# Seven computed chunks per image instead of five, with one bank for transposed taps and two for the turns

## The chip, the cores and the metric

The kernel runs on one core of a Trainium2 chip, in float32. The metric is the device time of one execution in microseconds (us), lower is better. The engines are PE (TensorE, matrix products into PSUM banks), DVE (VectorE), ACT (ScalarE), POOL (GpSimd, which here only issues gathers) and SP (SyncE, which issues the other DMAs). Each runs its own list of instructions in a fixed order, and they wait for one another by semaphores.

## The reference

Sixteen images of 64 channels and 64 x 64 pixels pass through two residual blocks. The first has a depthwise 3 x 3 convolution whose kernels are computed per image; the second has a deformable 3 x 3 convolution:

```python
x = x + _L0_conv_ref(_gn(x), ...)   # 1x1, per-image depthwise 3x3, y * tanh(softplus(y)), 1x1
x = x + _L1_conv_ref(_gn(x), ...)

# _L1_conv_ref:
offset = _conv2d(x, w_off, b_off)                     # 18 values per pixel
mask = jax.nn.sigmoid(_conv2d(x, w_mask, b_mask))     # 9 values per pixel
xd = _deform_conv(x, offset, mask, w_def)             # 9 taps, each bilinear from 4 gathered pixels
cat = jnp.concatenate([xd, offset, mask], axis=1)
z = jnp.einsum('bihw,oi->bohw', cat, w_1x1[:, :, 0, 0]) + b_1x1[None, :, None, None]
return jax.nn.silu(z * inv[None, :, None, None] + (bn_beta - bn_mean * inv)[None, :, None, None])
```

## The kernel before

**Chunks.** An image is 8 chunks (`NCH`) of 512 pixels. Chunk g of image b has number q = 8 b + g. While the deformable convolution of image b is sampled chunk by chunk, the work that prepares images b + 1 and b + 2 is done in between.

**Sampling by gathers.** For each of the nine taps of a chunk POOL issues four indirect DMAs (L505), each of which fetches, for 128 pixels, the 2 x 2 patch of the table into `gat`. DVE multiplies a tap by its bilinear weights (L1367) and sums the corners (L1346, into `pairs`, the ninth tap into `single`). Two taps make a pair. PE transposes it (`transposes`, L690) into `tap_ps`, ACT copies that to `val` (L1035), and PE multiplies it by the weights into `z_ps` (`product`, L696). At the chunk's end ACT applies the Silu (L1045) and DVE adds the result to x (`finish`, L1408). `gat` holds one chunk: POOL may fetch tap k of chunk q only when PE has transposed the corresponding pair of chunk q - 1; the waits stand at k = 0, 2, 4, 6 and 7 (`THROTTLE`).

**The computed tap.** In some chunks (`HATS`: 0 to 4, in image 0 `HATS0`: 3 and 4; internally "hat") the ninth tap isn't gathered but computed from a coarse part of the table that SP loads once for each image. Such a chunk has 32 gathers instead of 36. In the chunk ahead of it, PE spreads a coordinate or the mask over all partitions three times (`hat_y` L740, `hat_x` L747, `hat_mask` L754, here called the three spreads, all in `xh_ps`), DVE subtracts (`hat_part`, L1378) and weighs (`hat_weigh`, L1385), and at that chunk's end it writes five selections (`hat_select`, L1394). In the chunk itself ACT makes four maps of line weights (`hat_rows`), and PE does four **turns** (`hat_up`, L771): five matmuls of 128 x 512 each, into one bank. Float32 matmuls stand as two in the trace, so a turn is x10. DVE multiplies each turn by its line weights (`hat_post`, L1401), and PE adds that to `z_ps` (`hat_out`). Turn t + 1 waits for `hat_post` of turn t, since all turns share the bank `yo_ps`.

**Order.** Tables written out by hand set the order of the work. An entry is (units, step): the step is done when that many taps of the chunk have passed. `PLAN_BLOCK0` serves chunks 1 to 3 (first block of the next image: `convolve`, `project`, `residual`), `PLAN_NORM` chunk 4 (group norm), `PLAN_PREPARE` chunks 5 to 7. Chunks 5 and 6 make offsets (`offsets`, L645), pixel coordinates (`to_pixels`, L660, into `yo_ps`) and the table (`to_table`, L612) of the next image; chunk 7 its points and, for the image after it, the depthwise kernels (`kernel_taps` L548, `kernels` L1193) and hidden layer (`hidden`, L569). `PLAN_HAT` places the steps of a computed tap and `PLAN_NEXT_HAT` those ahead of it; each engine takes from them the steps that it has. PE takes a pair's transposes at even taps, as soon as DVE has summed both.

**Banks.** `tap_ps` has two banks, used in turn by the pairs; `yo_ps` serves turns and pixels, `xh_ps` the spreads.

## Time and profile before

| | us |
|---|---|
| median of 3 runs | 5573.58 |
| lowest, highest | 5561.91, 5580.89 |
| profiled execution, its own time | 5569.03 |
| its span | 5567.2 |

| engine | busy in the span |
|---|---|
| DVE | 80% |
| PE | 76% |
| POOL | 74%, without the time between its issues |
| ACT | 45% |

The profile shows one execution. Its page gives sums over the whole run; the stretches (windows) give the same for a part of it; the timeline shows each instruction with the idle time of the engine before it and what ended that. PEclk is the granted share of PE's full clock of 2.4 GHz; it is 1.0 or 0.5 at any moment. Image 9 stands for the others below: it begins at 3203.84 us and ends at 3542.68 us, by DVE's copies of the chunks' weights (L1355).

### The profile page before, as it was taken

How to read it: one execution, taken by the hardware profiler on the slowest of the kernel's cores; microseconds unless marked ns; L12 is line 12 of the kernel's file. 1: busy time of each engine (PE TensorE's matmuls, PEld its weight loads, DVE VectorE, ACT ScalarE, POOL GpSimd, SP SyncE). 2: the span in 40 equal slices, each digit the busy share in tenths (PEclk: the TensorE clock that was granted, in tenths of full speed). 3: DMA queues.
4: the chain of work that ended last, by engine and by line, in shares of the span. 5: the costliest groups of instructions: out<-in, count | busy, mean ns of one | idle time of the engine just before them, and what ended most of it. 6: DMA issues, size and time to landing. Idle time of an engine off the chain costs nothing.

```text
span 5567.2 us, 43350 instructions
## 1 busy us (share of the span) xinstructions
PE 4232.8 (76%) x13878; PEld 1852.8 (33%) x13878; DVE 4433.4 (80%) x5166; ACT 2478.1 (45%) x3420; POOL 4109.3 (74%) x4307
## 2 busy tenths in 40 slices
PE   8586777777777787777877778787787777778682
PEld 3233333333333333333333333333333333333231
DVE  5887869779697887978879797786978878788664
ACT  3354445445444444445544454454444444445221
POOL 1777777777777777777777777777777777777776
PEclk8686868879687786878868688696877868778685
...
GB/s 106 103 118 135 106 132 122 126 130 112 143 106 133 122 111 140 107 132 123 120 135 106 132 123 123 132 107 148 107 130 123 111 144 107 132 115 119 122 108 100
DMA packets 284052, 675.58 MB, mean 121 GB/s; under 512 B 77215, under 2 KB 119082, under 8 KB 281578
## 3 DMA queue, kind: packets, MB, share of 16 engines
...
## 4 chain that ended last, share of the span: by engine, by line
DVE 29%; POOL 28%; PE 26%; issue 13%; DMA 3%; ACT 1%; DVEq 0%; POOLq 0%; ACTq 0%; SPq 0%
POOL gat L505 28%; PE yo_ps L771 14%; DVE conv_ps L1237 7%; DVE gat L1367 5%; DVE pairs L1346 5%; DVE hat_s L1394 3%; DMA gat<-patch_table,ixu 3%; PE z_ps L696 3%; PE tap_ps L690 2%; DVE hat_wy L1401 1%; DVE xb L1258 1%; PE conv_ps L569 1%; DVE stat L1260 1%; PE xh_ps L754 1%; DVE conv_ps L1234 1%
## 5 line engine op out<-in xcount | busy, mean ns | idle before, releaser
L505 POOL DMA_INDIRECT gat<-patch_table,ixu x4300 | 4101.3, 954 | 1445.6 <-issue 1292.9
L771 PE MATMUL yo_ps<-hat_s,hat_image 128*128 128x512 f32 x3080 | 1660.9, 694 | 472.4 <-DVE hat_wy L1401 453.4
L1367 DVE TENSOR_TENSOR gat<-gat,wgt_ps 128x1024 f32<-128x1024 f32 x1075 | 1303.2, 1215 | 635.3 <-DMA gat<-patch_table,ixu 629.0
L1346 DVE TENSOR_REDUCE pairs<-gat 128x256 f32<-128x1024 f32 x1024 | 1239.7, 1211 | 0.0
L771 PEld LDWEIGHTS yo_ps<-hat_s,hat_image 128*128 128x128 f32 x3080 | 659.4, 223 | 1372.8 <-issue 871.5
L1035 ACT ACTIVATE val<-tap_ps 128x512 f32<-128x512 f32 x512 | 303.5, 593 | 1100.1 <-PE tap_ps L690 1099.7
L690 PE MATMUL tap_ps<-ident,pairs 128*128 128x128 f32 x2048 | 395.6, 325 | 470.4 <-DVE pairs L1346 470.3
L1237 DVE SCALAR_TENSOR_TENSOR conv_ps<-xh,kb,conv_ps 128x1024 f32<-128x1024 f32 x480 | 617.6, 1287 | 12.7
L690 PEld LDWEIGHTS tap_ps<-ident,pairs 128*128 128x128 f32 x2048 | 266.9, 163 | 759.5 <-DVE pairs L1346 618.3
L696 PE MATMUL z_ps<-val,w_pair 128*64 128x256 f32 x2048 | 425.2, 502 | 10.2 <-ACT val L1035 2.1
L645 PE MATMUL conv_ps<-np,w_om 128*41 128x512 f32 x1440 | 394.3, 706 | 39.4 <-ACT cat L994 39.4
L1075 ACT ACTIVATE hat_h<-xh_ps,hat_c 128x512 f32<-128x512 f32 x77 | 52.9, 688 | 800.3 <-PE xh_ps L747 800.3
L1401 DVE TENSOR_TENSOR hat_wy<-yo_ps,hat_wy 128x512 f32<-128x512 f32 x308 | 211.4, 686 | 215.0 <-PE yo_ps L771 210.8
L569 PE MATMUL conv_ps<-n_z,w_in 64*128 64x512 f32 x224 | 211.1, 1095 | 66.8 <-ACT n_z L899 60.3
L1394 DVE SCALAR_TENSOR_TENSOR hat_s<-hat_g,hat_c,xh_ps 128x512 f32<-128x512 f32 x385 | 259.6, 740 | 0.0
L991 ACT ACTIVATE cat<-conv_ps,vec 32x512 f32<-32x512 f32 x121 | 82.1, 679 | 326.4 <-PE conv_ps L645 322.4
L1059 ACT ACTIVATE hat_wy<-hat_wy,one_c 128x512 f32<-128x512 f32 x308 | 222.3, 722 | 10.0
L1057 ACT ACTIVATE hat_wy<-hat_d,hat_c 128x512 f32<-128x512 f32 x308 | 217.5, 706 | 0.0
L696 PE MATMUL z_ps<-hat_wy,w_hat 128*64 128x256 f32 x1232 | 202.1, 408 | 0.0
L645 PEld LDWEIGHTS conv_ps<-np,w_om 128*41 128x41 f32 x1440 | 97.4, 137 | 300.4 <-issue 254.6
L696 PEld LDWEIGHTS z_ps<-val,w_pair 128*64 128x64 f32 x2048 | 120.0, 161 | 182.6 <-issue 137.1
L612 PE MATMUL conv_ps<-ident,np 128*128 128x128 f32 x480 | 112.0, 371 | 85.6 <-ACT rec L970 85.6
...
## 6 DMA issues: line engine op xcount, KB each, us to landing
gat<-patch_table,ixu POOLq DMA_INDIRECT x4300
...
patch_table<-rec SPq DMA_DIRECT2D x120, 256.0 KB, 2.4
...
out<-n_z SPq DMA_DIRECT2D x128, 128.0 KB
...
```

The source lines that it names most:

```text
L505: pool.indirect_dma_start(gat[:, k, t * 2 * REC:(t + 1) * 2 * REC], None, table_rows, bass.IndirectOffsetOnAxis(ixu[:, i, k, t:t + 1], 0)) ...
L569: pe.matmul(hidden_ps(n, j)[:, :], w_in[C:, :], n0[C:, j, :], start=True, stop=True).then_inc(xh_mm, 1)
L645: m = pe.matmul(om_ps[C * j:C * j + OM, :], w_om[:, i, :], inner(np1, 0, 128, (s * 2 + j) * ROWS + 2 * (i // 3), i % 3), start=(i == 0), s ...
L690: m = pe.transpose(tap_ps[p % 2][:, t * 128:(t + 1) * 128], pairs[:, p, t, :] if p < PAIRS else single[:, t, :], ident[:, :])
L696: m = pe.matmul(z_ps[C * j:C * j + C, 0:CH // 2], weights, columns[:, j * CH // 2:(j + 1) * CH // 2], start=start, stop=stop)
L771: m = pe.matmul(hat_sum[:, :], hat_image[:, i, t, :], hat_s[:, i, :], start=(i == 0), stop=(i == HI - 1))
L1035: act.activation(val[:, p % 2, :], tap_ps[p % 2][:, :], ACT.Copy).then_inc(tap_done, 1)
L1237: dve.scalar_tensor_tensor(acc, src, kb[:, k:k + 1], acc, ALU.mult, ALU.add).then_inc(conv_sum, 1)
L1346: dve.tensor_reduce(total, gat[:, k, :].rearrange("p (t x c h) -> p t c x h", t=TILES, x=2, h=2), mybir.AxisListType.XY, ALU.add).then_inc ...
L1367: dve.tensor_tensor(patch, patch, wk.rearrange("p (n h) -> p n h", h=2).unsqueeze(2).to_broadcast([128, TILES * 2, C, 2]), ALU.mult).then_ ...
L1394: dve.scalar_tensor_tensor(hat_s[:, i, :], hat_g[:, :], hat_c[:, i:i + 1], hat_rows_ps[:, :], ALU.is_equal, ALU.mult).then_inc(hat_chosen, 1)
L1401: dve.tensor_tensor(hat_wy[:, t, :], hat_sum[:, :], hat_wy[:, t, :], ALU.mult).then_inc(hat_scaled, 1)
```

## The change

More chunks are computed: 0 to 6 of each image, and 3 to 6 of image 0. All transposed pairs go to one bank, `tap_ps[0]`, so a pair's transposes now wait for ACT's copy of the pair before. The other bank, `tap_ps[1]`, joins `yo_ps` for the turns: even turns use `yo_ps`, odd ones `tap_ps[1]`, and turn t waits for `hat_post` of turn t - 2. Pixels stay in `yo_ps`, and only even turns mind them. In a chunk without a computed tap the product of the last pair now comes ahead of the transposes of `single`. The tables are written anew: turns 0 and 1 at units 1 and 2, turns 2 and 3 at 5 and 6, and in chunks 5 to 7 offsets, table, pixels and points at other units.

```diff
@@ -44,8 +44,8 @@
 PXC = 2 * KK + KK
 GRID_X, GRID_Y = OM, OM + 1
 CROW = OM + 2
-HATS0 = (3, 4)
-HATS = (0, 1, 2, 3, 4)
+HATS0 = (3, 4, 5, 6)
+HATS = (0, 1, 2, 3, 4, 5, 6)
 HG = 7
 HT = 4
 HI = 5
@@ -65,15 +65,15 @@
 )
 PLAN_NORM = ((1, "project"), (3, "residual"), (4, "group_mean"), (5, "group_var"), (6, "normalise"), (8, "finish"))
 PLAN_PREPARE = (
-    ((1, "last_row"), (1, "offsets 0"), (2, "to_table 0"), (2, "x_stats 0"), (3, "to_table 1"), (4, "offsets 1"), (4, "to_pixels 0"),
-     (5, "to_table 2"), (5, "x_stats 1"), (6, "to_table 3"), (7, "to_pixels 1"), (8, "to_table 4"), (8, "finish")),
-    ((1, "offsets 2"), (2, "to_table 5"), (2, "points 0"), (3, "offsets 3"), (3, "to_pixels 2"), (4, "points 1"), (4, "to_table 6"),
-     (5, "x_stats 2"), (5, "to_table 7"), (6, "points 2"), (6, "to_pixels 3"), (7, "x_stats 3"), (8, "finish")),
-    ((1, "x_mean"), (1, "points 3"), (2, "x_var"), (2, "points 4"), (2, "next_indices"), (3, "x_norm"), (3, "points 5"),
+    ((1, "last_row"), (2, "offsets 0"), (2, "to_table 0"), (2, "x_stats 0"), (3, "to_table 1"), (4, "to_pixels 0"), (4, "to_table 2"),
+     (5, "offsets 1"), (5, "x_stats 1"), (6, "to_table 3"), (7, "to_table 4"), (8, "to_pixels 1"), (8, "finish")),
+    ((2, "offsets 2"), (2, "to_table 5"), (2, "points 0"), (4, "to_pixels 2"), (4, "points 1"), (4, "to_table 6"),
+     (5, "offsets 3"), (5, "x_stats 2"), (6, "points 2"), (6, "to_table 7"), (7, "x_stats 3"), (8, "to_pixels 3"), (8, "finish")),
+    ((1, "x_mean"), (2, "points 3"), (2, "x_var"), (3, "points 4"), (3, "next_indices"), (3, "x_norm"), (4, "points 5"),
      (4, "hidden_units"), (5, "kernel_taps"), (6, "kernels"), (6, "hidden 0"), (7, "hidden 1"), (8, "hidden 2"), (8, "finish"), (KK, "hidden 3")),
 )
-PLAN_HAT = ((1, "hat_rows"), (1, "hat_up 0"), (3, "hat_post 0"), (3, "hat_up 1"), (5, "hat_post 1"), (5, "hat_out 0"), (5, "hat_up 2"),
-            (6, "hat_out 1"), (7, "hat_post 2"), (7, "hat_up 3"), (8, "hat_out 2"), (KK, "hat_post 3"))
+PLAN_HAT = ((1, "hat_rows"), (1, "hat_up 0"), (2, "hat_up 1"), (3, "hat_post 0"), (4, "hat_post 1"), (5, "hat_out 0"), (5, "hat_up 2"),
+            (6, "hat_out 1"), (6, "hat_up 3"), (7, "hat_post 2"), (8, "hat_post 3"), (8, "hat_out 2"))
 PLAN_NEXT_HAT = ((1, "hat_y"), (3, "hat_part"), (4, "hat_x"), (6, "hat_mask"), (8, "hat_weigh"), (KK, "hat_select"))
 
 
@@ -361,7 +361,7 @@
 
             return C if n % 2 == 0 else 0
 
-        hat_sum, hat_rows_ps = yo_ps, xh_ps
+        hat_sums, hat_rows_ps = (yo_ps, tap_ps[1]), xh_ps
 
         def inner(buf, lo, hi, r0, c0):
 
@@ -686,8 +686,9 @@
             def transposes(q, p):
 
                 pe.wait_ge(summed, KK + taps_before(q) + min(2 * p + 2, KK))
+                pe.wait_ge(tap_done, copies_before(q) + p + 2)
                 for t in range(TILES if p < PAIRS else TILES // 2):
-                    m = pe.transpose(tap_ps[p % 2][:, t * 128:(t + 1) * 128], pairs[:, p, t, :] if p < PAIRS else single[:, t, :], ident[:, :])
+                    m = pe.transpose(tap_ps[0][:, t * 128:(t + 1) * 128], pairs[:, p, t, :] if p < PAIRS else single[:, t, :], ident[:, :])
                 m.then_inc(tap_mm, 1)
 
             def to_z(weights, columns, start=False, stop=False):
@@ -723,9 +724,9 @@
                         if k > 2:
                             product(q, k // 2 - 2)
                     if k == KK - 1:
+                        product(q, PAIRS - 1)
                         if not has_hat(q):
                             transposes(q, PAIRS)
-                        product(q, PAIRS - 1)
                         last_products(b, g)
 
             def hat_y(q):
@@ -762,13 +763,14 @@
                         pe.wait_ge(cleared, 3)
                         pe.wait_ge(om_done, NCH)
                     pe.wait_ge(hat_chosen, HI * h + HI)
-                if h + t > 0:
-                    pe.wait_ge(hat_scaled, HT * h + t)
-                if after_px:
-                    pe.wait_ge(px_done, after_px.pop())
-                ups[0] = HT * h + t + 1
+                if h > 0 or t > 1:
+                    pe.wait_ge(hat_scaled, HT * h + t - 1)
+                if t % 2 == 0:
+                    if after_px:
+                        pe.wait_ge(px_done, after_px.pop())
+                    ups[0] = HT * h + t + 1
                 for i in range(HI):
-                    m = pe.matmul(hat_sum[:, :], hat_image[:, i, t, :], hat_s[:, i, :], start=(i == 0), stop=(i == HI - 1))
+                    m = pe.matmul(hat_sums[t % 2][:, :], hat_image[:, i, t, :], hat_s[:, i, :], start=(i == 0), stop=(i == HI - 1))
                 m.then_inc(hat_mm, 1)
 
             def hat_out(q, t):
@@ -1032,12 +1034,12 @@
                     if k % 2 == 0 and k > 0:
                         p = k // 2 - 1
                         act.wait_ge(tap_mm, GROUPS + groups_before(q) + p + 1)
-                        act.activation(val[:, p % 2, :], tap_ps[p % 2][:, :], ACT.Copy).then_inc(tap_done, 1)
+                        act.activation(val[:, p % 2, :], tap_ps[0][:, :], ACT.Copy).then_inc(tap_done, 1)
                     if k == KK - 1 and not has_hat(q):
                         act.wait_ge(tap_mm, GROUPS + groups_before(q) + GROUPS)
                         for h in range(2):
                             act.activation(val[0:C, PAIRS % 2, :].rearrange("p (t h x) -> p t h x", h=2, x=128)[:, :, h, :],
-                                           tap_ps[PAIRS % 2][C * h:C * h + C, 0:CH // 2].rearrange("p (t x) -> p t x", x=128), ACT.Copy).then_inc(tap_done, 1)
+                                           tap_ps[0][C * h:C * h + C, 0:CH // 2].rearrange("p (t x) -> p t x", x=128), ACT.Copy).then_inc(tap_done, 1)
                 if hi < KK:
                     return
                 act.wait_ge(z_mm, q + 1)
@@ -1398,7 +1400,7 @@
                 h = hats_before(q)
                 dve.wait_ge(hat_mm, HT * h + t + 1)
                 dve.wait_ge(hat_lines, 2 * (HT * h + t) + 2)
-                dve.tensor_tensor(hat_wy[:, t, :], hat_sum[:, :], hat_wy[:, t, :], ALU.mult).then_inc(hat_scaled, 1)
+                dve.tensor_tensor(hat_wy[:, t, :], hat_sums[t % 2][:, :], hat_wy[:, t, :], ALU.mult).then_inc(hat_scaled, 1)
 
             def finish(b, g):
 
```

In chunk 2 of an image, PE's list was, from the first spread for the next chunk to turn 2:

```order
L740 MATMUL xh_ps<-cat,hat_sel 128x512
L771 MATMUL yo_ps<-hat_s,hat_image 128x512 x5
L589 MATMUL conv2_ps<-uc,w_out 128x512 x2
L690 MATMUL tap_ps0<-ident,pairs 128x128 x4
L771 MATMUL yo_ps<-hat_s,hat_image 128x512 x5
L747 MATMUL xh_ps<-cat,hat_sel 128x512
L690 MATMUL tap_ps1<-ident,pairs 128x128 x4
L696 MATMUL z_ps<-cat,w_cat 64x256 x2
L696 MATMUL z_ps<-val,w_pair 64x256 x2
L696 MATMUL z_ps<-hat_wy,w_hat 64x256 x2
L771 MATMUL yo_ps<-hat_s,hat_image 128x512 x5
```

and is now:

```order
L741 MATMUL xh_ps<-cat,hat_sel 128x512
L773 MATMUL yo_ps<-hat_s,hat_image 128x512 x5
L589 MATMUL conv2_ps<-uc,w_out 128x512 x2
L773 MATMUL tap_ps1<-hat_s,hat_image 128x512 x5
L691 MATMUL tap_ps0<-ident,pairs 128x128 x4
L748 MATMUL xh_ps<-cat,hat_sel 128x512
L691 MATMUL tap_ps0<-ident,pairs 128x128 x4
L697 MATMUL z_ps<-cat,w_cat 64x256 x2
L697 MATMUL z_ps<-val,w_pair 64x256 x2
L697 MATMUL z_ps<-hat_wy,w_hat 64x256 x2
L773 MATMUL yo_ps<-hat_s,hat_image 128x512 x5
```

Turn 1 has moved ahead of the first pair's transposes; the second pair's transposes now stand between it and turn 2, with the second spread.

In chunk 5, from chunk 4's last product to the pixels and the first product of its own, PE's list was (L602 is the table's last row, L645 offsets, L612 table, L690 or L691 transposes, L660 pixels):

```order
L696 MATMUL z_ps<-hat_wy,w_hat 64x256 x2
L602 MATMUL conv2_ps<-ident,np1 97x128 x2
L645 MATMUL conv2_ps<-np1,w_om 41x512 x12
L612 MATMUL conv2_ps<-ident,np1 128x128 x4
L690 MATMUL tap_ps0<-ident,pairs 128x128 x4
L612 MATMUL conv2_ps<-ident,np1 128x128 x4
L645 MATMUL conv2_ps<-np1,w_om 41x512 x12
L660 MATMUL yo_ps<-to_px,cat 128x27 x8
L690 MATMUL tap_ps1<-ident,pairs 128x128 x4
L696 MATMUL z_ps<-cat,w_cat 64x256 x2
```

and is now:

```order
L697 MATMUL z_ps<-hat_wy,w_hat 64x256 x2
L741 MATMUL xh_ps<-cat,hat_sel 128x512
L773 MATMUL yo_ps<-hat_s,hat_image 128x512 x5
L602 MATMUL conv2_ps<-ident,np1 97x128 x2
L645 MATMUL conv2_ps<-np1,w_om 41x512 x12
L612 MATMUL conv2_ps<-ident,np1 128x128 x4
L773 MATMUL tap_ps1<-hat_s,hat_image 128x512 x5
L691 MATMUL tap_ps0<-ident,pairs 128x128 x4
L612 MATMUL conv2_ps<-ident,np1 128x128 x4
L660 MATMUL yo_ps<-to_px,cat 128x27 x8
L612 MATMUL conv2_ps<-ident,np1 128x128 x4
L748 MATMUL xh_ps<-cat,hat_sel 128x512
```

A spread for chunk 6 and two turns have come in ahead of the first pair's transposes, and the second offsets (L645) have moved behind the first products. Turns 2 and 3 follow later in the chunk.

## Rows read from the trace of the kernel before

**Rows 1.** The page: busy time by engine, and the gathers among the costliest groups.

```profile
PE 4232.8 (76%) x13878; PEld 1852.8 (33%) x13878; DVE 4433.4 (80%) x5166; ACT 2478.1 (45%) x3420; POOL 4109.3 (74%) x4307
...
L505 POOL DMA_INDIRECT gat<-patch_table,ixu x4300 | 4101.3, 954 | 1445.6 <-issue 1292.9
```

**Rows 2.** Waits of POOL, whole run: us in total, times, longest.

```profile
POOL gat L505 <- PE tap_ps L690: 42.0, 59, 4.4
```

**Rows 3.** Windows, chunks and image 9: us; PE, PEld, DVE, ACT, POOL busy (x); PEclk.

```profile
3203.84:3245.88 42.04, 36.40 (x102) 14.81 (x102) 36.82 (x39) 23.00 (x31) 31.68 (x35) 0.82 0.60 157
3245.88:3290.97 45.09, 34.83 (x102) 14.27 (x102) 41.15 (x44) 21.26 (x28) 34.11 (x37) 0.85 0.37 108
3290.97:3334.61 43.64, 33.00 (x102) 13.54 (x102) 41.16 (x44) 21.28 (x28) 32.98 (x36) 0.92 0.37 109
3334.61:3379.72 45.11, 34.83 (x102) 14.27 (x102) 41.17 (x45) 21.27 (x28) 34.09 (x36) 0.85 0.35 108
3379.72:3411.82 32.10, 28.39 (x85) 12.29 (x86) 26.32 (x35) 16.72 (x17) 24.44 (x26) 0.89 0.37 109
3411.82:3441.44 29.62, 24.56 (x120) 11.38 (x122) 24.25 (x26) 15.95 (x26) 22.48 (x24) 0.81 0.42 133
3441.44:3487.01 45.57, 35.81 (x162) 18.18 (x158) 30.88 (x43) 16.33 (x29) 34.51 (x36) 0.69 0.49 146
3487.01:3542.68 55.67, 37.87 (x101) 17.05 (x100) 35.08 (x54) 22.23 (x36) 42.15 (x45) 0.53 0.46 123
3203.84:3542.68 338.84, 265.68 (x872) 115.79 (x872) 276.83 (x319) 158.04 (x218) 256.44 (x271) 0.78 0.43 124
```

**Rows 4.** Waits in chunk 7 of image 9.

```profile
DVE gat L1367 <- DMA gat<-patch_table,ixu: 12.0, 5, 4.0
```

**Rows 5.** Timeline of DVE, chunk 2 of image 9: start, us, instruction, idle before.

```profile
3313.12 1.21 DVE L1346 TENSOR_REDUCE pairs<-gat 128x256 f32<-128x1024 f32 x1
...
3330.72 0.69 DVE L1401 TENSOR_TENSOR hat_wy<-yo_ps,hat_wy 128x512 f32<-128x512 f32 x1 [2.03 <-PE yo_ps L771]
3331.32 3.37 DVE L1394 SCALAR_TENSOR_TENSOR hat_s<-hat_g,hat_c,xh_ps 128x512 f32<-128x512 f32 x5
```

**Rows 6.** Timeline of PE, chunk 2 of image 9: turns 0 and 1.

```profile
3292.17 4.56 PE L771 MATMUL yo_ps<-hat_s,hat_image 128*128 128x512 f32 x10
...
3305.43 7.23 PE L771 MATMUL yo_ps<-hat_s,hat_image 128*128 128x512 f32 x10 [6.54 <-DVE hat_wy L1401]
3312.59 1.12 PE L747 MATMUL xh_ps<-cat,hat_sel 43*128 43x512 f32 x2
```

**Rows 7.** Timeline of PE, chunk 5 of image 9: offsets, table, transposes, pixels.

```profile
3414.43 5.35 PE L645 MATMUL conv_ps<-np,w_om 128*41 128x512 f32 x24
3419.72 0.75 PE L612 MATMUL conv_ps<-ident,np 128*128 128x128 f32 x4
3420.30 0.60 PE L690 MATMUL tap_ps<-ident,pairs 128*128 128x128 f32 x4
...
3433.33 1.96 PE L660 MATMUL yo_ps<-to_px,cat 41*128 41x27 f32 x16
```

**Rows 8.** Window of PE's small matmuls in chunks 5 and 6; clock after the engines.

```profile
3437.20:3451.30 14.10, 13.04 (x54) 8.60 (x53) 8.00 (x9) 5.44 (x11) 10.75 (x12) 0.50 0.54 172
```

**Rows 9.** Timeline of PE, chunk 7 of image 9: transposes, kernel taps, hidden.

```profile
3511.26 1.11 PE L690 MATMUL tap_ps<-ident,pairs 128*128 128x128 f32 x4 [2.56 <-DVE pairs L1346]
...
3514.41 4.00 PE L548 MATMUL conv_ps<-hcx,kg_w 128*128 128x1 f32 x18
3518.86 3.75 PE L569 MATMUL conv_ps<-n_z,w_in 64*128 64x512 f32 x4 [0.46 <-DVE kb L1193]
```

**Rows 10.** Timeline of DVE, chunk 7 of image 9.

```profile
3491.32 1.22 DVE L1367 TENSOR_TENSOR gat<-gat,wgt_ps 128x1024 f32<-128x1024 f32 x1 [4.01 <-DMA gat<-patch_table,ixu]
...
3518.45 0.17 DVE L1193 TENSOR_TENSOR kb<-conv_ps,kg_b 128x9 f32<-128x9 f32 x1 [1.43 <-PE conv_ps L548]
...
3542.07 0.68 DVE L1408 TENSOR_TENSOR n_z<-n_z,xb 64x512 f32<-64x512 f32 x1 [6.21 <-ACT n_z L1045]
```

## Prediction

> **What bounds the kernel now.** I read the page's busy line first: DVE 80%, PE 76%, POOL 74% [rows 1]. That hides the bound. POOL's gathers are busy 4101.3 us and stand 1292.9 us in "issue" [rows 1], together 5394.2 of 5567.2 us; over the whole run POOL waits only 42.0 us for PE's transposes [rows 2]. One gather thus costs 5394.2 / 4300 = 1.254 us. An image with five computed chunks has 268 gathers, 336.1 us; image 9 took 338.84 [rows 3]. POOL paces the kernel.
>
> The stretches of image 9 show the second resource [rows 3]. They begin where DVE copies a chunk's weights. POOL needs 40.1 us for a computed chunk (32 gathers) and 45.1 for another (36). Chunks 0 to 3 take DVE 42.0 to 45.1, chunks 4 and 5 only 32.1 and 29.6: DVE and PE fall behind POOL by some 16 us over four chunks and win it back in two light ones. In chunks 6 and 7 DVE has caught up and waits for gathers, 12.0 us of chunk 7 [rows 4]. The patch buffer holds about one chunk, which is how far POOL can lead. So the kernel is fast as long as DVE and PE together need less than POOL over an image, and the change touches both sides.
>
> **What the change takes from POOL.** 2 more chunks in 15 images and 2 more in image 0 are computed: 32 chunks x 4 gathers x 1.254 us = 160.5 us, 10.0 us an image. That is all there is to gain while POOL bounds; then an image takes 260 x 1.254 = 326.1 us.
>
> **What it puts on DVE and PE.** A computed chunk loses two DVE passes of 1.21 us (multiply and sum of the last tap). It gains four turn products of 0.69, and the chunk before it one pass each for part and weight (0.6) and five selections, 3.37 [rows 5]. That is about +5.1 us of DVE for each, 10.2 an image on 276.8 [rows 3]: not yet over the line. On PE it gains four turns of 4.56 us at the full clock [rows 6], 3 spreads of 1.1, and 4 products of some 0.6 for the 2 that it loses, about 22 us; at the half clock nearly twice that. PE was busy 265.7 of 338.8 us [rows 3], so with two more such chunks it is busy some 310.
>
> Since both engines work in a fixed order, I walk the chunks in the new order.
>
> *Chunk 5.* This is the term that decides. It was the lightest chunk; PE spent 24.6 of 29.6 us on two conversions of offsets, five table chunks and two of pixels [rows 3]. At the full clock PE's list now is: 4 turns at 4.4 from start to start = 17.6; three spreads 3.2; two offsets at 5.3 = 10.6; two pixel groups at 1.9 = 3.8; five table chunks and the last row at about 0.6 = 3.4; four transposes and nine products at 0.58 = 7.5 [rows 7]. Sum 46.1 us. All its inputs are ready early, so PE runs through. DVE ends when turn 3 and then the mask spread are done (39.5), and then weighs 0.6, sums tap 7 1.1 and selects 3.3: 44.6 us. That is 15.0 more than before, and more than POOL's 40.1.
>
> The clock comes on top. PE was busy 13.04 of 14.10 us in a stretch of transposes, products and pixels in chunks 5 and 6, and was granted 0.50 throughout, 1.2 of 2.4 GHz [rows 8]. Chunk 5 now has two such stretches between turns and offsets: to_table 1 to product 0, and from the mask spread to the chunk's end. A turn after such a stretch is slower: 7.23 against 4.56 us after 6.54 us of idling [rows 6]. Bounds: 44.6 us if none is lost, 49 if both stretches and the turns behind them lose 2 us each. I take 46.5, **+16.9**.
>
> By the Trainium skill, "TensorE: Matmul & The Clock Gate", Part 4: PE-mode transpose, transposes do not bring up the full clock as other matmuls do. The row on the 14.10 us agrees, though other small matmuls stand in it too. By that rule chunk 5 would take the upper bound, 49 us, and without it 44.6.
>
> *Chunk 6* gets four turns, and no next selection behind it. PE starts 1.4 us late; turns 0, offsets, table and turn 1 end at 16, turn 3 at 36.6; DVE's last product and sum follow: 38.5 at the full clock, 43.6 with the same losses. Before it was held by gathers to 45.6. I take 40.5, **-5.1**.
>
> *Chunk 4* now prepares chunk 5: +4.6 us of DVE; but turn 1 no longer stands ahead of the group mean. Walked: turn 3 ends at 28.6, then the mask, and 5.0 us of weighing, summing and selecting: 34.8; with slow turns 38.4. I take 36.0, **+3.9**.
>
> *Chunks 1 to 3.* DVE's own work is 41.2 us, the chunks took 45.1, 43.6 and 45.1 [rows 3]; the rest is DVE's wait for turns, as 2.03 us for turn 3 [rows 5]. This is what the pairs are to remove. Turns 0 and 1 now run back to back and end at 11.7 us, before DVE needs them. But PE then idles, but for one spread, until DVE has summed tap 3: the sum starts at 22.15 us [rows 5], 22.75 with the earlier product, and ends at 23.9. Then come transposes, products, turn 2 (26.2 to 30.6), turn 3 (to 35.6) and the mask (36.7), and DVE ends at 41.9. After an idle of 7.9 us I expect the half clock, as turn 1 had before [rows 6]: 1.7 us more for the small matmuls and 1.5 to 2.7 for turn 2. Then it ends at 45.6. The slow turn has only moved from turn 1, where DVE had time, to turn 2, where it has none. Bounds 41.9 and 45.6; I take 44.6, **0**. Chunk 0, without residual, 41.0, **-1.0**.
>
> *Chunk 7* is held by gathers no longer. Before, the transposes of taps 2 and 3 began at 3511.26, 24.2 us into it, of which DVE had waited 4.01 for gathers: without that, 20.2. From there to DVE's addition of the kernel bias went 3518.45 - 3511.26 = 7.2 us at the half clock, and on to the end of the image 24.2 (three hidden pairs at 3.75 us, then the last sum, ScalarE and a 6.21 us wait of DVE) [rows 9, 10]. The new order puts the last transpose behind the product before it, 1.2 more: a transpose and its copies in a row. 20.2 + 7.2 + 24.2 + 1.2 = 52.8, **-2.9**. Only a warm PE would shorten it.
>
> **Sum.** 41.0 + 3 x 44.6 + 36.0 + 46.5 + 40.5 + 52.8 = 350.6 us an image, against 338.8: +11.8. It is over POOL's 326.1, so POOL now waits for PE. For images 0 to 14 that is +177. The last image has no work for a next one: it runs at POOL's pace, saves its 10 us, and lets POOL's larger lead, by estimate 13 us (between 0 and 25), run off: -23. So 5569.0 + 177 - 23 = 5723 us. The median of the runs is 4.6 us above the profiled one: 5728.
>
> The single bank for transposes costs nothing: ScalarE's copy of a pair (0.6 us) is done long before the next pair's sums, two taps of 2.26 us later. It would show only where PE is late and pairs follow one another.
>
> **Rivals.**
> *All at the full clock.* If PE, denser now, keeps it through chunks 0 to 6: 39.5 + 3 x 41.9 + 34.8 + 44.6 + 38.5 + 52.8 = 335.9, or -2.9 an image: 5569 - 44 - 23 + 5 = 5507, faster. For it: in chunks 2 and 4 the granted share was already 0.92 and 0.89. Against: every idle of over 6 us and the small matmuls cost it [rows 6, 8]. It decides at an average of 338 us an image. If chunk 7 also came to the full clock (hidden pairs at half of 3.75) POOL would bound again at 326.1 and the time would be near 5400.
>
> *All losses at once.* Chunks 42, 3 x 45.6, 38.4, 49, 43.6, 52.8 = 362.6: +357 - 23 + 5, or about 5908.
>
> *The two cancel.* 338 to 340 us an image. It needs chunks 1 to 3 at 43 and chunk 5 at 44.6: 5545 to 5590, no difference.
>
> *The second bank does not help.* If DVE's waits for turns stay as before everywhere, chunks 0 to 3 keep their 42 to 45 us: that is my forecast within 1 us, so it is not told apart by time, only by whose turn DVE waits for.
>
> **How the numbers follow.** My forecast, slower by 1% or more, has 0.60; all losses 0.08; cancelled 0.11; full clock 0.21, with POOL-bound in it at 0.03. Range: from 5510, near the full clock, to 5830, where the average image is 358 us; outside I leave some 0.10 each. About 0.3% (17 us) is what a measurement can tell. Faster 0.21, within 0.3% 0.09, slower 0.70.
>
> **What would show it.** Right: POOL's wait for PE's transposes rises from 42 us to over 250; DVE's waits for gathers in chunks 5 to 7 vanish; chunk 5 takes 45 to 49 us and is PE's; in chunks 1 to 3 PE's idle before turn 1 is gone and one before the second pair's transposes stands there; DVE ends an image with over 10 us of waiting for ScalarE. Wrong: a clock over 0.85 with chunk 5 under 44 us, POOL still without waits, or chunk 7 under 48 us.

## The result, and the profile after

The changed kernel takes 6133.54 us (median of 4 runs, 6132.76 to 6134.91) against 5569.53 us of the kernel before in the same runs: ratio 1.1011, 95% interval 1.099 to 1.1032. It is slower, as forecast, but by 564 us where the forecast said some 160. The time lies above the range.

The page after, busy time by engine and the gathers' group, answers to [rows 1]:

```profile
PE 4941.4 (81%) x15670; PEld 2149.9 (35%) x15670; DVE 4582.3 (75%) x5454; ACT 2725.8 (44%) x3740; POOL 3968.1 (65%) x4179
...
L505 POOL DMA_INDIRECT gat<-patch_table,ixu x4172 | 3960.1, 949 | 2150.6 <-issue 1193.2
```

POOL's wait for PE, whole run (us in total, times, longest), answers to [rows 2]:

```profile
POOL gat L505 <- PE tap_ps L691: 843.3, 254, 6.2
```

POOL's own work as listed fell from 5394.2 to 3960.1 + 1193.2 = 5153.3 us, but it now waits 843.3 us for PE's transposes, where it waited 42.0. (Part of the fall is only in the listing: a gather that waits for PE has no "issue" entry of 0.3 us. 270 gathers have none now, 60 had none before.) The bound has moved from POOL to PE and DVE. The windows of image 9, columns as in [rows 3], show where:

```profile
3546.62:3589.40 42.78, 35.70 (x94) 14.91 (x94) 36.92 (x38) 19.50 (x27) 29.19 (x32) 0.78 0.57 147
3589.40:3640.88 51.48, 37.38 (x102) 15.47 (x102) 41.34 (x45) 21.38 (x28) 30.23 (x33) 0.77 0.28 84
3640.88:3692.12 51.24, 37.20 (x102) 15.40 (x102) 41.34 (x45) 21.38 (x28) 30.20 (x33) 0.77 0.28 85
3692.12:3743.32 51.20, 37.18 (x102) 15.40 (x102) 41.33 (x44) 21.37 (x28) 30.28 (x33) 0.77 0.28 85
3743.32:3787.37 44.05, 38.87 (x114) 16.21 (x114) 31.00 (x43) 25.64 (x28) 30.24 (x33) 0.81 0.33 99
3787.37:3834.91 47.54, 47.41 (x192) 21.91 (x192) 29.06 (x35) 23.15 (x39) 30.22 (x33) 0.93 0.40 121
3834.91:3874.89 39.98, 39.89 (x168) 18.00 (x164) 30.64 (x45) 19.43 (x31) 28.18 (x30) 0.96 0.39 122
3874.89:3927.14 52.25, 36.74 (x117) 17.86 (x116) 34.68 (x54) 21.89 (x35) 39.67 (x41) 0.57 0.46 129
```

The image takes 380.5 us, 41.7 more than before. Chunks 5, 6 and 7 came out as forecast (47.5, 40.0, 52.3 for 46.5, 40.5, 52.8), and chunk 0 within 2 us. Chunks 1 to 3 take 51.3 us each where I had 44.6 and an upper bound of 45.6, and chunk 4 takes 44.1 for 36.0. In chunks 1 to 3 neither engine is full: DVE works 41.3 of 51.2 us, PE 37.2. So the two wait for each other by turns. Two of DVE's three largest waits, whole run, columns as for POOL's:

```profile
DVE hat_wy L1403 <- PE yo_ps L773: 368.8, 104, 12.1
DVE xb L1260 <- PE conv_ps L589: 336.1, 60, 6.4
```

The second is new: 60 times 5.6 us, four in each image, for the projection (L589) that the residual (L1260) needs. In the kernel before it was 17.4 us in all, 13 times. From the end of chunk 2 of image 9 into chunk 3 (DVE starts chunk 3 at 3692.12) the timelines read, PE first:

```profile
3686.92 0.66 PE L691 MATMUL tap_ps<-ident,pairs 128*128 128x128 f32 x4
...
3688.97 0.66 PE L691 MATMUL tap_ps<-ident,pairs 128*128 128x128 f32 x4 [0.38 <-DVE pairs L1348]
3689.55 0.65 PE L697 MATMUL z_ps<-val,w_pair 128*64 128x256 f32 x4
3693.64 1.12 PE L697 MATMUL z_ps<-val,w_pair 128*64 128x256 f32 x4 [3.43 <-ACT val L1037]
...
3695.54 2.07 PE L741 MATMUL xh_ps<-cat,hat_sel 43*128 43x512 f32 x2
3697.55 6.65 PE L773 MATMUL yo_ps<-hat_s,hat_image 128*128 128x512 f32 x10
3704.03 1.88 PE L589 MATMUL conv_ps<-uc,w_out 128*128 128x512 f32 x4
```

ACT, same stretch:

```profile
3687.61 0.60 ACT L1037 ACTIVATE val<-tap_ps 128x512 f32<-128x512 f32 x1 [9.32 <-PE tap_ps L691]
3688.23 1.28 ACT L930 ACT_TABLE_LOAD   x1
3689.52 1.15 ACT L930 ACTIVATE uc<-uc,one_c 128x1024 f32<-128x1024 f32 x1
3690.75 1.28 ACT L940 ACT_TABLE_LOAD   x1
3692.04 1.06 ACT L940 ACTIVATE uc<-uc 128x1024 f32<-128x1024 f32 x1
3693.00 0.58 ACT L1037 ACTIVATE val<-tap_ps 128x512 f32<-128x512 f32 x1
```

DVE, at the start of chunk 3:

```profile
3698.11 1.21 DVE L1348 TENSOR_REDUCE pairs<-gat 128x256 f32<-128x1024 f32 x1
3705.09 0.75 DVE L1260 SCALAR_TENSOR_TENSOR xb<-conv_ps,vec,xb 128x512 f32<-128x512 f32 x1 [5.77 <-PE conv_ps L589]
```

The fourth pair's transposes are done at 3689.6, but ACT can't copy them: it does the activation's ln (L930) and tanh (L940) first, with a table load of 1.28 us for each, 4.8 us together. PE stands 3.43 us for the copy. After that the granted clock is 0.50 (window 3693.60 to 3700.00), and back at 1.00 from 3705: the spread takes 2.07 us for 1.12, turn 0 6.65 for 4.56. Behind them stands the projection, and behind that DVE. In the kernel before ACT had the same queue:

```profile
3325.64 0.60 ACT L1035 ACTIVATE val<-tap_ps 128x512 f32<-128x512 f32 x1 [3.74 <-PE tap_ps L690]
3326.26 1.28 ACT L928 ACT_TABLE_LOAD   x1
...
3330.07 1.06 ACT L938 ACTIVATE uc<-uc 128x1024 f32<-128x1024 f32 x1
3331.88 0.60 ACT L1035 ACTIVATE val<-tap_ps 128x512 f32<-128x512 f32 x1 [0.76 <-PE tap_ps L690]
```

There turn 3 stood between the two transposes. It gave ACT 6.2 us from copy to copy, enough for 4.8 of activation and 0.6 of copy, and ACT even waited 0.76. The new table puts turn 3 ahead of the third pair's transposes, so the two pairs follow within 2.05 us, and the cover is gone.

My theory after the result: **ACT's queue** (ln and tanh between the two copies) costs some 6 us in each of chunks 1 to 4. Rivals: **too much work** (the two more computed chunks wear down POOL's lead and the rest follows), **the banks** (one bank for transposes makes pairs wait for ACT's copies), and **turn 0 ahead of the projection**, by its place alone.

### The profile page after: what moved, and what is told of

Read it like the earlier page. It is cut to its first block, busy times and chain, and to the rows that moved or that the text cites. A ratio compares the mean times of both kernels' runs of the same rounds, so it can differ in the third digit from the quotient of the medians.

```text
span 6131.3 us, 48264 instructions
## 1 busy us (share of the span) xinstructions
PE 4941.4 (81%) x15670; PEld 2149.9 (35%) x15670; DVE 4582.3 (75%) x5454; ACT 2725.8 (44%) x3740; POOL 3968.1 (65%) x4179
## 4 chain that ended last, share of the span: by engine, by line
PE 59%; DVE 24%; ACT 7%; issue 5%; POOL 4%; DMA 0%; DVEq 0%; ACTq 0%; POOLq 0%; SPq 0%
PE yo_ps L773 18%; PE tap_ps L773 10%; PE z_ps L697 9%; PE conv_ps L645 5%; DVE gat L1369 5%; DVE pairs L1348 5%; DVE conv_ps L1239 4%; PE tap_ps L691 4%; POOL gat L505 4%; PE conv_ps L569 3%; PE xh_ps L741 2%; PE xh_ps L755 2%; DVE hat_wy L1403 2%; DVE xb L1260 1%; DVE stat L1262 1%
## 5 line engine op out<-in xcount | busy, mean ns | idle before, releaser
L505 POOL DMA_INDIRECT gat<-patch_table,ixu x4172 | 3960.1, 949 | 2150.6 <-issue 1193.2
L773 PE MATMUL yo_ps<-hat_s,hat_image 128*128 128x512 f32 x2180 | 1280.1, 746 | 0.9 <-issue 0.9
L773 PE MATMUL tap_ps<-hat_s,hat_image 128*128 128x512 f32 x2180 | 982.5, 597 | 0.0
L691 PE MATMUL tap_ps<-ident,pairs 128*128 128x128 f32 x2048 | 397.9, 327 | 667.4 <-DVE pairs L1348 665.9
L773 PEld LDWEIGHTS yo_ps<-hat_s,hat_image 128*128 128x128 f32 x2180 | 509.3, 245 | 798.6 <-issue 798.6
L691 PEld LDWEIGHTS tap_ps<-ident,pairs 128*128 128x128 f32 x2048 | 269.3, 163 | 1019.3 <-DVE pairs L1348 821.9
L773 PEld LDWEIGHTS tap_ps<-hat_s,hat_image 128*128 128x128 f32 x2180 | 403.2, 190 | 496.9 <-issue 485.3
L1403 DVE TENSOR_TENSOR hat_wy<-tap_ps,hat_wy 128x512 f32<-128x512 f32 x218 | 149.2, 684 | 319.4 <-PE tap_ps L773 319.4
L1396 DVE SCALAR_TENSOR_TENSOR hat_s<-hat_g,hat_c,xh_ps 128x512 f32<-128x512 f32 x545 | 367.4, 740 | 0.0
L645 PE MATMUL conv_ps<-np,w_om 128*41 128x512 f32 x1440 | 342.2, 627 | 0.0
L1260 DVE SCALAR_TENSOR_TENSOR xb<-conv_ps,vec,xb 128x512 f32<-128x512 f32 x120 | 89.1, 743 | 336.1 <-PE conv_ps L589 336.1
L697 PE MATMUL z_ps<-hat_wy,w_hat 128*64 128x256 f32 x1744 | 338.6, 474 | 0.0
L1061 ACT ACTIVATE hat_wy<-hat_wy,one_c 128x512 f32<-128x512 f32 x436 | 314.6, 722 | 14.1
L1059 ACT ACTIVATE hat_wy<-hat_d,hat_c 128x512 f32<-128x512 f32 x436 | 307.8, 706 | 0.0
```

The lines of the kernel that those rows point to most:

```text
L505: pool.indirect_dma_start(gat[:, k, t * 2 * REC:(t + 1) * 2 * REC], None, table_rows, bass.IndirectOffsetOnAxis(ixu[:, i, k, t:t + 1], 0)) ...
L645: m = pe.matmul(om_ps[C * j:C * j + OM, :], w_om[:, i, :], inner(np1, 0, 128, (s * 2 + j) * ROWS + 2 * (i // 3), i % 3), start=(i == 0), s ...
L691: m = pe.transpose(tap_ps[0][:, t * 128:(t + 1) * 128], pairs[:, p, t, :] if p < PAIRS else single[:, t, :], ident[:, :])
L697: m = pe.matmul(z_ps[C * j:C * j + C, 0:CH // 2], weights, columns[:, j * CH // 2:(j + 1) * CH // 2], start=start, stop=stop)
L773: m = pe.matmul(hat_sums[t % 2][:, :], hat_image[:, i, t, :], hat_s[:, i, :], start=(i == 0), stop=(i == HI - 1))
L1061: act.activation(hat_wy[:, t, :], hat_wy[:, t, :], ACT.Relu, bias=one_c[:, :], scale=-1.0).then_inc(hat_lines, 1)
```

## The experiments

Medians over images 1 to 13 of the time of each chunk, in us. Each ratio is to runs of the kernel before taken beside that kernel; their medians lie between 5557 and 5570 us, so times of different rows are compared to some 12 us.

| kernel | 0 | 1 | 2 | 3 | 4 | 5 | 6 | 7 | us | ratio to before, 95% | POOL waits for tap_ps |
|---|---|---|---|---|---|---|---|---|---|---|---|
| before | 41.2 | 45.1 | 43.6 | 45.1 | 32.1 | 29.7 | 45.4 | 55.6 | 5569.53 | | 42.0 |
| after | 42.8 | 51.5 | 51.2 | 51.2 | 44.0 | 47.5 | 40.0 | 52.2 | 6133.54 | 1.099 to 1.1032 | 843.3 |
| e1_early_ln | 42.0 | 44.6 | 44.5 | 44.4 | 39.3 | 47.5 | 38.6 | 51.7 | 5759.04 | 1.0311 to 1.0372 | 434.5 |
| e2_five_hats | 41.9 | 50.6 | 51.2 | 51.2 | 36.3 | 30.3 | 45.4 | 59.1 | 5955.43 | 1.0663 to 1.0725 | 480.5 |
| e3_old_tables | 41.4 | 44.9 | 46.3 | 44.7 | 37.5 | 51.8 | 47.9 | 52.4 | 5963.52 | 1.0678 to 1.074 | 658.9 |
| e6_project_first | 42.6 | 45.3 | 44.6 | 46.2 | 40.6 | 47.5 | 39.9 | 52.1 | 5836.59 | 1.045 to 1.0512 | 510.4 |
| f4_turn3_late | 42.1 | 44.7 | 46.8 | 45.0 | 39.6 | 48.0 | 38.0 | 51.9 | 5791.04 | 1.0372 to 1.0433 | 472.3 |
| f1_five_early | 41.8 | 44.5 | 44.4 | 44.4 | 34.6 | 31.5 | 45.2 | 59.1 | 5674.67 | 1.0164 to 1.0223 | 162.6 |
| f3_one_bank_early | 45.5 | 44.6 | 44.5 | 44.6 | 40.2 | 47.5 | 40.5 | 52.1 | 5843.50 | 1.0466 to 1.0527 | 519.2 |
| f5_fill | 39.6 | 43.2 | 42.0 | 43.2 | 39.4 | 47.6 | 38.6 | 51.8 | 5660.70 | 1.0139 to 1.0198 | 339.2 |
| f2_six_early | 42.3 | 44.9 | 44.5 | 44.4 | 34.6 | 41.1 | 45.0 | 52.2 | 5695.67 | 1.0212 to 1.0273 | 273.1 |
| b1_hat6 | 41.6 | 43.6 | 45.2 | 43.6 | 30.8 | 39.2 | 54.8 | 51.7 | 5733.93 | 1.0274 to 1.0359 | 332.7 |
| b3_hat6_fill | 41.2 | 43.6 | 45.2 | 43.6 | 30.8 | 39.2 | 54.8 | 51.7 | 5723.99 | 1.0265 to 1.0329 | 330.7 |
| b2_fill | 41.7 | 43.6 | 45.1 | 43.6 | 30.8 | 30.4 | 45.4 | 55.4 | 5551.52 | 0.9965 to 0.9996 | 45.0 |

### ln and tanh ahead of the copies (e1_early_ln)

```diff
 PLAN_BLOCK0 = (..., (6, "exp"),
-               (7, "ln"), (8, "tanh"), (8, "finish"))
+               (6, "ln"), (6, "tanh"), (8, "finish"))
```

(The same in `PLAN_FIRST`.)

> The changed kernel with one thing moved: ScalarE's ln and tanh of the next image's first block come at unit 6, right behind exp, instead of at 7 and 8, so ahead of its copy of the third transposed pair. Theory Q (queue): in chunks 0 to 3 the third pair's transposes stand behind turns 2 and 3, ln and tanh with their table loads (4.8 us) then stand between ScalarE's copies of the third and the fourth pair, PE's last product waits 3.43 us for the fourth copy, and the next chunk's projection comes late for the residual, for which DVE waits 5.8 us in each of chunks 1 to 4. Then the 3.4 us wait goes, DVE's wait shrinks to 2 to 3 us, an image falls from 379 to about 365 us and the time to some 5930 us. Theory L (load): PE simply has too much work with seven computed chunks; then the time stays within 1% of 6134 us.

Measured 5759.04 us: one edit of two numbers takes back 374 of the 564 us, nearly twice the 200 that I had expected. Chunks 1 to 3 fall to 44.5, chunk 4 to 39.3. ACT and PE at the same place, end of chunk 2 of image 9, ACT first:

```profile
3446.57 1.28 ACT L940 ACT_TABLE_LOAD   x1
3447.86 1.06 ACT L940 ACTIVATE uc<-uc 128x1024 f32<-128x1024 f32 x1
3452.29 0.60 ACT L1037 ACTIVATE val<-tap_ps 128x512 f32<-128x512 f32 x1 [3.37 <-PE tap_ps L691]
3454.33 0.60 ACT L1037 ACTIVATE val<-tap_ps 128x512 f32<-128x512 f32 x1 [1.45 <-PE tap_ps L691]
```

PE there:

```profile
3456.93 1.12 PE L741 MATMUL xh_ps<-cat,hat_sel 43*128 43x512 f32 x2 [0.86 <-DVE hat_s L1396]
3457.98 4.56 PE L773 MATMUL yo_ps<-hat_s,hat_image 128*128 128x512 f32 x10
3462.37 1.88 PE L589 MATMUL conv_ps<-uc,w_out 128*128 128x512 f32 x4
```

ACT now waits for PE at both copies, the spread and turn 0 run at the full clock, and the projection starts 5.6 us into the chunk instead of 11.9. ACT's queue is shown as the cause of the loss in chunks 1 to 3, and of 374 of the 405 us by which the forecast missed.

### Five computed chunks in the new order (e2_five_hats)

```diff
-HATS0 = (3, 4, 5, 6)
-HATS = (0, 1, 2, 3, 4, 5, 6)
+HATS0 = (3, 4)
+HATS = (0, 1, 2, 3, 4)
```

> The changed kernel with the computed chunks of before (0 to 4, in image 0 only 3 and 4); banks, tables and orders stay changed. Theory Q: chunks 1 to 3 stay at 51 us, since their order is what costs; chunks 5 and 6 are light again, and POOL's 336 us and DVE's and PE's own some 340 to 345 us an image are near each other: 5640 to 5720 us. Theory L: the load is that of before, so the time is that of before, 5570 us.

Measured 5955.43 us. With the old amount of work chunks 1 to 3 still take 50.6 to 51.2 us. Too much work doesn't explain them. My sum for the whole, 5640 to 5720 us, was far too low: an image takes 366 us by the table, where I had put 340 to 345.

### The old tables with the new banks (e3_old_tables)

```diff
-PLAN_HAT = ((1, "hat_rows"), (1, "hat_up 0"), (2, "hat_up 1"), ...
+PLAN_HAT = ((1, "hat_rows"), (1, "hat_up 0"), (3, "hat_post 0"), (3, "hat_up 1"), ...
```

(And `PLAN_PREPARE` as before.)

> The changed kernel, seven computed chunks and the new banks, but with the tables of before for the turns and for chunks 5 to 7 (turns at units 1, 3, 5 and 7). Theory Q: the third pair's transposes stand ahead of turn 3 again; chunks 1 to 3 return to some 45 us, an image takes about 352 to 360 us, and the time is 5740 to 5860 us. Theory L: within 1% of 6134 us, or slower, because chunks 5 and 6 lose their packing.

Measured 5963.52 us. Chunks 1 to 3 fall back to 45: the order made the loss there, not the banks. But chunks 5 and 6 take 51.8 and 47.9 us, 12 us more than in the new order, and with that the time is above the 5740 to 5860 us that I had expected: the new tables, those of the turns and of chunks 5 to 7 together, are worth having where chunks 5 and 6 are computed.

### The projection ahead of turn 0 (e6_project_first)

```diff
+    first, plan = plan[:1] if plan[0][1] == "project" else (), plan[1:] if plan[0][1] == "project" else plan
-    return by_unit(PLAN_NEXT_HAT[0:1] if has_hat(q + 1) else (), PLAN_HAT[0:2] if has_hat(q) else (), plan,
+    return by_unit(PLAN_NEXT_HAT[0:1] if has_hat(q + 1) else (), first, PLAN_HAT[0:2] if has_hat(q) else (), plan,
```

> The changed kernel with the projection of the next image (two matmuls, L589) ahead of turn 0 on PE in chunks 1 to 4, instead of behind it; nothing else moves. Theory Q: DVE's 5.8 us wait for it goes to 0 to 1 us, turn 0 has time to spare, an image falls from 379 by some 20 us and the time to about 5830 us. Theory L: PE's work is the same, so at most 1% is gained.

Measured 5836.59 us, as expected. PE still waits 3.4 us for the copy (58 times, 197.7 us in all), but DVE's 5.8 us for the projection shrinks to 0.3. So the late copy hurts mainly because turn 0, slow after it, stands ahead of what DVE needs. Breaking either link of the chain takes back most of the loss, 297 us here and 374 with ln and tanh moved.

### Turn 3 back behind the third pair (f4_turn3_late)

```diff
-            (6, "hat_out 1"), (6, "hat_up 3"), (7, "hat_post 2"), (8, "hat_post 3"), (8, "hat_out 2"))
+            (6, "hat_out 1"), (7, "hat_post 2"), (7, "hat_up 3"), (8, "hat_out 2"), (KK, "hat_post 3"))
```

> The changed kernel, ln and tanh at 7 and 8 as in it, but turn 3 at unit 7, behind the third pair's transposes, and its product at the chunk's end. Theory Q: ScalarE's copy of the third pair and with it ln and tanh come earlier, the 3.4 us wait of the last product and most of the 5.8 us of DVE for the projection go, and chunks 1 to 3 take 45 to 47 us: 5770 to 5900 us. Theory that only ln's and tanh's own place matters: within 1% of 6134 us.

Measured 5791.04 us, with ln and tanh where the change has them. It restores the cover: turn 3 again stands between the two pairs' transposes, PE's 3.4 us wait for the copy is gone, and 342 us come back, where moving ln and tanh gave 374. That is the same cause seen from PE's side.

### What is left of the loss: the number of computed chunks (f1_five_early, f2_six_early)

Both have e1_early_ln's edit, and `HATS` (0 to 4) with `HATS0` (3, 4), or (0 to 4, 6) with (3, 4, 6).

> The changed kernel with ln and tanh at unit 6 and with the computed chunks of before (0 to 4). What is left of the order's cost is seen without the load of two more computed chunks. Theory Q: chunks 1 to 3 take 44.5 us as in the run with early ln alone, which is what they took before the change; the kernel is paced by POOL again, but chunk 7, where DVE first catches up with the gathers, is some 3 us longer through the new places of points and of the last product: 5580 to 5640 us. Theory L, that load and order multiply: below 5570 us.

> The changed kernel with ln and tanh at unit 6, ahead of the copies of the third and fourth pair, and computed chunks 0 to 4 and 6 (image 0: 3, 4, 6), against seven (5759 us) and five (5675 us) in the same form. Theory (each computed chunk more in 5 or 6 costs DVE and PE about 42 us / 15 per image more than POOL gives back): halfway, 5715 us. Rival (chunk 6 is cheap and chunk 5, whose pixels stand between its turns, dear): 5680 us or less, with chunk 5 at about 32 us and chunk 6 at 46 to 50.

Measured 5674.67 and 5695.67 us; with seven it is 5759.04. The sixth costs 21 us, the seventh 63 (28 and 55 by the ratios). Six came out 19 us below my 5715: chunk 4 stays at 34.6 as long as chunk 5 isn't computed. The surprise is f1_five_early, 1.9% slower than before with the same work and above the 5580 to 5640 us that I had expected. POOL paces it again, but POOL now waits 162.6 us for transposes, where it waited 42.0. Of that, 150 us stand ahead of the gathers of tap 4 in chunks 2, 3 and 4, and these wait for the third pair's transposes of the chunk before (`THROTTLE`). In chunk 2 of image 9 (from 3395.21 us), PE and then POOL:

```profile
3434.41 0.66 PE L691 MATMUL tap_ps<-ident,pairs 128*128 128x128 f32 x4
3435.34 0.94 POOL L505 DMA_INDIRECT gat<-patch_table,ixu  x1 [4.65 <-PE tap_ps L691]
```

The third pair's transposes start 39.2 us into the chunk. Before, with turn 3 behind them, it was 34.0 (3324.95 us in the kernel before). So by these rows turn 3 ahead of the third pair costs a second time: the 120.6 us more that POOL waits are about the 107 us by which this kernel is slower than the one before. No run moved turn 3 back with five computed chunks, so this is read from the trace and not shown by an experiment.

### The banks (f3_one_bank_early)

e1_early_ln with the banks of before: all turns in `yo_ps`, transposes in turn in two banks. The waits of the turns and ACT's copies change with them; a part of the edit:

```diff
-        hat_sums, hat_rows_ps = (yo_ps, tap_ps[1]), xh_ps
+        hat_sums, hat_rows_ps = (yo_ps, yo_ps), xh_ps
...
-                pe.wait_ge(tap_done, copies_before(q) + p + 2)
```

> The changed kernel with ln and tanh at unit 6, but with the banks of before: all turns in yo_ps, transposed pairs in two banks; the tables stay changed. Theory Q (order decides, banks hardly): turn 1 waits for turn 0's product and turn 3 for turn 2's, 1 to 2 us a chunk later at the end: 5760 to 5900 us. Rival B (one bank for transposed pairs costs): it is faster than 5759 us.

Measured 5843.50 us, 84 us slower than with the new banks. Whatever the single bank for transposes costs is less than what the pair of banks for turns gains. Together they are worth 3.5 us in chunk 0 and 1 to 2 us in chunks 4 and 6. In chunks 1 to 3 the pair is worth nothing (44.6, 44.5, 44.6 against 44.6, 44.5, 44.4). With the new tables the banks are the sound half of the change; in the order of before they weren't tried alone.

### Added matmuls in PE's idle (f5_fill)

e1_early_ln with seven more matmuls of 128 x 512 (four in chunk 0), in chunks 0 to 3 of images 1 to 14, just ahead of the second pair's transposes; what they write is overwritten.

```diff
+                if p == 1 and has_hat(q) and NCH <= q < (B - 1) * NCH and q % NCH < 4:
+                    pe.wait_ge(tap_done, copies_before(q) + p + 2)
+                    for _ in range(4 if q % NCH == 0 else 7):
+                        pe.matmul(tap_ps[0][:, :], ident[:, :], ..., start=True, stop=True)
```

> The changed kernel with ln and tanh at unit 6, and with 7 extra matmuls of 128x512 (4 in chunk 0) in PE's 7 us idle ahead of the second pair's transposes in chunks 0 to 3 of images 1 to 14. Their output is overwritten; they are there to keep the clock. If the half clock after that idle costs what the prediction took (1.7 us on small matmuls and 1.5 to 2.7 on turn 2), chunks 1 to 3 fall from 44.5 to about 42.3 us, and the time from 5759 by 14 x 4 x 2 = 110 us to 5650. If the clock costs nothing there, the time stays or grows by some us.

Measured 5660.70 us, 98 us less with more work. PE in chunk 2 of image 9:

```profile
3370.47 7.61 PE L691 MATMUL tap_ps<-kg_w,ident 128*128 128x512 f32 x14
3378.05 0.66 PE L695 MATMUL tap_ps<-ident,pairs 128*128 128x128 f32 x4
...
3380.24 4.56 PE L777 MATMUL yo_ps<-hat_s,hat_image 128*128 128x512 f32 x10
```

After the idle the transposes took 1.11 and turn 2 6.09 us in the changed kernel (at 3670.77 and 3674.77 us), and turn 2 5.08 us in e1_early_ln; here 0.66 and 4.56. Chunk 2 falls from 44.5 to 42.0, the 41.9 that I had worked out for a clock that is never lost; chunks 1 and 3 fall to 43.2. The slow turn 2, "where DVE has no time", was real.

### The kernel before with a sixth computed chunk, and with added matmuls (b1_hat6, b2_fill, b3_hat6_fill)

```diff
-HATS0 = (3, 4)
-HATS = (0, 1, 2, 3, 4)
+HATS0 = (3, 4, 6)
+HATS = (0, 1, 2, 3, 4, 6)
```

and, for the other two, twelve added matmuls (result overwritten) behind the first pair's transposes in chunks 1 to 3, where PE idles ahead of turn 1.

> The kernel before (its banks, its tables) with one computed chunk more per image: 0 to 4 and 6 (image 0: 3, 4 and 6). It has 264 gathers per image where before has 268, so POOL's floor falls from 336 to 331 us per image. Theory (POOL bounds the kernel before, and the change lost only by what its new order does): POOL is still the engine that everybody waits for; 333 us per image, about 5490 us, ratio 0.985, and POOL's wait for tap_ps stays under 120 us. Rival (chunks 5 to 7 have no room for the three spreads and the four turns, which share yo_ps with the pixels): chunks 5 and 6 rise by 10 us together, 345 us per image, about 5650 us, and POOL waits over 250 us for tap_ps.

> The kernel before with added work: 12 matmuls of 128x512, whose result is overwritten, behind the first pair's transposes in chunks 1 to 3 of images 1 to 14, where PE idles 6.5 us ahead of turn 1. Theory (POOL bounds before, PE's slow turn 1 is cover): turn 1 falls from 7.2 to 4.6 us, chunks 1 to 3 don't shrink, 5567 us, ratio 1.000 within 0.003. Rival (DVE and PE also bound chunks 1 to 3, at 45.1 where 32 gathers take 40): chunks 1 to 3 fall by 2 us each, about 5480 us, ratio 0.985. If the fill itself delays PE it is slower than 1.003.

> The kernel before with both: computed chunks 0 to 4 and 6, and the 12 added matmuls (result overwritten) in chunks 1 to 3 of images 1 to 14. If POOL still bounds the six-chunk form, the same time as that form alone, within 0.3% (about 5490 us). If its new bound is DVE or PE in chunks 1 to 3, another 1% less, about 5440 us.

b1_hat6 took 5733.93 us: my theory missed it by 244 us, and the rival was right in kind and too small. Chunks 5 and 6 rise by 19 us, chunk 7 gives 4 back. DVE's largest wait, whole run:

```profile
DVE hat_wy L1401 <- PE yo_ps L771: 561.8, 149, 18.9
```

The window of chunk 6 of image 9, columns as in [rows 3]:

```profile
3553.77:3608.58 54.81, 46.30 (x184) 20.51 (x184) 30.51 (x45) 20.48 (x34) 40.55 (x42) 0.89 0.40 122
```

PE's timeline there (L645 offsets, L660 pixels, L771 turn 1):

```profile
3571.26 5.35 PE L645 MATMUL conv_ps<-np,w_om 128*41 128x512 f32 x24 [3.25 <-ACT cat L994]
3576.54 1.96 PE L660 MATMUL yo_ps<-to_px,cat 41*128 41x27 f32 x16
3581.44 6.96 PE L771 MATMUL yo_ps<-hat_s,hat_image 128*128 128x512 f32 x10 [2.93 <-ACT px L999]
```

In the old order turn 1 stands behind the second offsets, which wait 3.25 us for ACT, and behind the pixels. Then it waits 2.93 us for ACT's copy of the pixels, whose bank it shares. DVE waits 17.60 us for it. How much of that is the order and how much the bank wasn't separated. The new tables and banks do the same chunk in 45.0 us (f2_six_early), but pay for it elsewhere. Here, too, I had summed engines and not walked their order.

b2_fill took 5551.52 us, ratio 0.9981. The added matmuls took 10.5 us, more than the idle that they were to fill, since one of 128 x 512 in float32 takes 0.87 us and not the half of it that I had assumed. Still they did to the clock what was expected, as the window of chunk 3 of image 9 shows:

```profile
3329.24:3372.86 43.62, 40.29 (x126) 17.07 (x126) 41.13 (x44) 21.27 (x28) 32.08 (x34) 1.00 0.35 106
```

and PE's timeline of chunk 2, turn 1:

```profile
3302.28 4.45 PE L775 MATMUL yo_ps<-hat_s,hat_image 128*128 128x512 f32 x10
```

A clock of 1.00 and a turn of 4.45 for 7.23 us bought 0.2%: POOL bounds the kernel before. b3_hat6_fill against b1_hat6 gives 0.2% as well, within the scatter. There POOL doesn't set the pace (it waits 330.7 us for PE), yet chunks 1 to 3 take 43.6, 45.2 and 43.6 us with the added matmuls and without; what holds them there I haven't taken apart. No version beat the kernel before by 0.3%.

## Why the prediction was right or wrong

**What bounds before: right.** b2_fill speeds up PE where it was slow and gains 0.2%, so POOL paces it. Of the gathers exactly 128 went, 4300 to 4172. Their price hardly moved: busy 949 ns each for 954, and 305 ns of issue in both, where there is any. So POOL's part shrank by some 180 us for the forecast's 160.5. None of it reached the time.

**Chunk 5: right.** 47.5 us, between 44.6 and 49, and PE is busy 47.41 of them. Why between, PE shows:

```profile
3808.47 1.11 PE L691 MATMUL tap_ps<-ident,pairs 128*128 128x128 f32 x4
3809.51 1.12 PE L697 MATMUL z_ps<-cat,w_cat 41*64 41x256 f32 x4
...
3811.47 6.79 PE L645 MATMUL conv_ps<-np,w_om 128*41 128x512 f32 x24
...
3829.71 0.66 PE L691 MATMUL tap_ps<-ident,pairs 128*128 128x128 f32 x4
3830.29 0.65 PE L697 MATMUL z_ps<-val,w_pair 128*64 128x256 f32 x4
```

Of the two light stretches the first fell to the half clock (1.11 for 0.60, and the offsets behind it 6.79 for 5.35), the second kept the full one. By the Trainium skill, "TensorE: Matmul & The Clock Gate", Part 4: PE-mode transpose, transposes don't bring up the full clock; the first stretch agrees, in the second the clock was there already and stayed.

**Chunks 6 and 7: right.** 40.0 and 52.3 us. DVE's wait for the kernel bias is 4.98 us for 1.43, and the one at the image's end 11.12 for 6.21 [rows 10], "over 10 us" as forecast:

```profile
3902.06 0.17 DVE L1195 TENSOR_TENSOR kb<-conv_ps,kg_b 128x9 f32<-128x9 f32 x1 [4.98 <-PE conv_ps L548]
...
3926.53 0.69 DVE L1410 TENSOR_TENSOR n_z<-n_z,xb 64x512 f32<-64x512 f32 x1 [11.12 <-ACT n_z L1047]
```

**Chunks 1 to 3: the step that failed.** The walk took each chunk by itself: it followed turns 0 to 3, the transposes and the spreads on PE and the passes on DVE. Then it let the last pair's product follow its transposes at once, and it began the next chunk with turn 0 and the projection at the full clock. On ACT it checked only the copy's length: "ScalarE's copy of a pair (0.6 us) is done long before the next pair's sums". What stood in ACT's queue between two copies it didn't look at, though the timeline of before showed 4.8 us of ln, tanh and table loads there, with 0.76 us to spare. The term was 6.7 us too small in each of three chunks. With ACT's queue out of the way (e1_early_ln) they take 44.5, the forecast's 44.6; with the clock kept as well (f5_fill) 42.0 to 43.2, near its lower bound.

**Chunk 4: wrong, half by the same step.** 44.1 against 36.0. Moving ln and tanh gives back 4.8; 39.3 us remain, 0.9 over my upper bound. In e1_early_ln turn 3 of chunk 4 ends 33.0 us into it, and not 28.6. The clock is most of that: it was granted at 0.51 from 3520 to 3527 us, four groups of small matmuls ahead of turn 2 took half a microsecond more each, and turn 2 took 6.77 us for 4.56:

```profile
3522.41 6.77 PE L773 MATMUL yo_ps<-hat_s,hat_image 128*128 128x512 f32 x10
```

I had put 1.2 us on the clock there (36.0 for 34.8).

**The sum.** Per image the miss is 3 x 6.7 + 8 = 28 us, and the other four chunks together stay within 2 us of the forecast. Image 0, where chunks 0 to 2 aren't computed, missed by only 14 (it lost 25.5 us for my 11.8). 14 x 28 + 14 = 406; measured 6133.54 - 5728 = 405. The 23 us for the end came out: the last image took 326.8 us, near POOL's 326.1 and 10.9 less than before, and image 14 lost 29.5 us where images 1 to 13 lost 40.1 in the mean. e1_early_ln, which is the change without that one fault, takes 5759 us, 31 us (0.5%) from the number that I gave. That it is so close is in part luck: chunk 4 is 3.3 us over the forecast, chunks 0 and 5 are 1.0 each, and chunks 6 and 7 are 1.9 and 1.1 under it.

**The chances.** "All losses at once" (5908 us) was the worst case that I had, and it too took its chunks from PE's walk. The range was too narrow on the side where a queue that I hadn't read could act. "The second bank does not help" held in chunks 1 to 3 and fell elsewhere: f3_one_bank_early puts the banks at 84 us, all outside chunks 1 to 3.

**The signs.** All the signs named for "right" came: POOL's wait over 250 us (843.3), no wait of DVE for gathers in chunks 5 to 7 of image 9, chunk 5 at 47.5 us and PE's, turn 1 without idle and 7.8 us of idle ahead of the second pair's transposes, 11.12 us for ScalarE at the image's end. None of those named for "wrong" came. They tested what the walk had in it, and none looked at what it left out.
